# Moving chain links, exponentials and head means of a linear-attention layer by one step in a two-layer transformer kernel

## The reference

```
u_sum = cumsum(u);  bar_u = (log_tau * prior_mu + u_sum) / (log_tau + t)
s_i = -sum(u * bar_u) / sqrt(d)
exp_s = exp(s_i - max(s_i));  E_t = cumsum(exp_s);  P_t = cumsum(s_i)
F_t, G_t, H_t = cumsum(exp_s * k v), cumsum(s_i * k v), cumsum(k v)
M = alpha * F_t + beta * G_t + gamma * H_t      # factors from gate, E_t, P_t
out = q M per head;  out = (out - mean) / sqrt(var + 1e-5);  h = h + out @ Wo.T
```

## Time and profile before

| | us |
|---|---|
| median of 3 runs | 579.2 (577.5 to 581.55) |
| the profiled execution's own time | 581.57 |
| its span, first to last instruction | 579.7 |
| PE busy | 522.0 (90%) |
| PE weight load busy | 495.8 (86%) |
| DVE busy | 382.7 (66%) |
| ACT busy | 256.1 (44%) |
| POOL busy | 226.5 (39%) |

### The profile page before, as it was taken

One profiled execution on the slowest core, in us unless ns is written; L12 is line 12 of the kernel. 1 busy time (PEld: TensorE's weight loads), 2 busy tenths in 40 slices (PEclk: granted clock), 3 DMA queues, 4 the chain that ended last, 5 costly groups with the idle time before them and its releaser, 6 DMA issues. The chain is left out here.

```text
span 579.7 us, 9772 instructions
## 1 busy us (share of the span) xinstructions
PE 522.0 (90%) x3430; PEld 495.8 (86%) x3430; DVE 382.7 (66%) x934; ACT 256.1 (44%) x531; POOL 226.5 (39%) x186
## 2 busy tenths in 40 slices
PE   5799878989999999999999699796687879999996
PEld 5799778989999999999999598585566778999995
DVE  1576748747666666665663966999764766466665
ACT  0347561335455445544651248754631255243432
POOL 1403102746557666765666023774432100021300
PEclk9899967989999999999999899989777799799999
DMA  8740001855566756755743340000202000000001
GB/s 340 258 204 1 2 0 31 320 173 172 180 225 216 276 196 236 253 222 199 246 169 94 97 150 2 0 2 1 75 1 75 1 0 2 2 0 1 2 0 62
DMA packets 22634, 65.03 MB, mean 112 GB/s; under 512 B 6432, under 2 KB 15008, under 8 KB 19776
## 3 DMA queue, kind: packets, MB, share of 16 engines
q1 hardware_dynamic: 20192, 59.55, 29.3%
q0 software_dynamic: 2400, 4.93, 2.5%
HBM read 55.50 MB, written 8.97 MB: 111 GB/s over the span
## 5 line engine op out<-in xcount | busy, mean ns | idle before, releaser
L726 POOL TENSOR_TENSOR w0l<-stage,w0h 128x768 fp32r<-128x768 f32 x34 | 62.5, 1839 | 81.4 <-ACT w0h L710 68.6
L683 PE MATMUL bank<-w0d,a0h 128*128 128x192 f32 x492 | 84.2, 329 | 1.3 <-DVE a0h L765 1.3
L683 PEld LDWEIGHTS bank<-w0d,a0h 128*128 128x128 f32 x492 | 80.8, 192 | 1.6 <-DVE a0h L765 1.6
L758 DVE TENSOR_SCALAR a0t<-bank 128x256 f32<-128x256 f32 (+1 forms) x114 | 50.8, 445 | 41.8 <-PE bank L663 41.5
L737 ACT ACTIVATE bank<-bank 128x256 f32<-128x256 f32 x96 | 35.3, 368 | 84.7 <-PE bank L663 80.7
L663 PE MATMUL bank<-XWh,w0h 128*128 128x256 f32 x192 | 56.1, 292 | 0.0
L663 PE MATMUL bank<-XWh,w0t 128*128 128x256 f32 x192 | 54.5, 284 | 0.0
L663 PE MATMUL bank<-XWh,w0l 128*128 128x256 f32 x192 | 53.9, 281 | 0.0
L663 PE MATMUL bank<-XWl,w0h 128*128 128x256 f32 x192 | 53.9, 281 | 0.0
L663 PE MATMUL bank<-XWl,w0t 128*128 128x256 f32 x192 | 53.9, 280 | 0.0
L446 PE MATMUL bank<-X,w1h 128*128 128x384 f32 x144 | 49.3, 343 | 2.2 <-DVE a1hf L601 2.2
(11 more groups left out here) (256 smaller groups left out, 1302.6 us busy)
## 6 DMA issues: line engine op xcount, KB each, us to landing
stage<-moe0w SPq DMA_DIRECT2D x18, 1536.0 KB, 7.4
w0d<-moe0d SPq DMA_DIRECT2D x18, 576.0 KB, 3.9
stage<-moe1w SPq DMA_DIRECT2D x4, 1056.0 KB, 5.1
marked_rows<-zero SPq DMA_DIRECT2D x4, 772.0 KB, 13.1
patch<-patches SPq DMA_DIRECT2D x4, 768.0 KB, 8.3
XR<-marked_rows SPq DMA_DIRECT2D x16, 192.0 KB, 3.6
G<-slots_out SPq DMA_DIRECT2D x6, 288.0 KB, 4.7
XR<-marked_rows SPq DMA_DIRECT2D x16, 65.0 KB, 3.9
```

The source lines that it names most:

```text
L683: last = nc.tensor.matmul(dst, A0["h"][qpar][:, fc, t * P:(t + 1) * P], W0[par]["down"][:, fc, :], start=(fc == these[0]), stop=(fc == the ...
L726: ins = engine.tensor_tensor(W0[par]["l"][:, mat, :], src, W0[par]["h"][:, mat, :].bitcast(F32), ALU.subtract)
L758: nc.vector.tensor_scalar(A0["t"][fc % 2][:, 0:width], bank[2 + fc % 2][:, 0:width], LIMIT, -LIMIT, ALU.min, ALU.max).then_inc(S0["clip_re ...
```

## The change

Some pieces of the stage stand elsewhere in the step loop; no instruction is added or taken away.

- Chain: `CHAIN` lists us4 ahead of et1 and us5 ahead of cum1. In steps, before: st1 in 0, et1 in 2, us4 in 3, cum1 and us5 in 4, st2 in 5, et2 in 6, cum2 in 7. Now: st1 in 0, us4 in 1, et1 and us5 in 2, cum1 in 3, st2 in 4, et2 in 6, cum2 in 7.
- ACT: `exps(1)` stands in step 1 instead of 2 and `exps(2)` in step 5 instead of 6, each ahead of `centred_squares` and the squares and roots of its step.
- DVE: `masks(g)` stands ahead of `head_variances` and `head_factors` of its step, and `head_means` directly behind `combine`, ahead of key factors, cosines and links.

```diff
-CHAIN = [("us", 0), ("us", 1), ("st", 0), ("us", 2), ("et", 0), ("us", 3), ("cum", 0), ("st", 1), ("et", 1),
-         ("us", 4), ("cum", 1), ("us", 5), ("st", 2), ("et", 2), ("cum", 2)]
+CHAIN = [("us", 0), ("us", 1), ("st", 0), ("us", 2), ("et", 0), ("us", 3), ("cum", 0), ("st", 1), ("us", 4),
+         ("et", 1), ("us", 5), ("cum", 1), ("st", 2), ("et", 2), ("cum", 2)]
-CHAIN_IN = ((7,), (), (8,), (9,), (10, 11), (12,), (13,), (14,))
+CHAIN_IN = ((7,), (8,), (9, 10), (11,), (12,), (), (13,), (14,))
 # ACT, step g
                 out_copies(outs)
+                if g in (1, 5):
+                    exps(g // 5 + 1)
                 if g in (5, 9):
                     centred_squares(g // 4 - 1)
                 if g in (6, 10):
                     head_deviations(g // 4 - 1)
-                if g in (2, 6):
-                    exps(g // 5 + 1)
 # DVE, step g
+                masks(g)
                 if g in (6, 10):
                     head_variances(g // 4 - 1)
                 if g == 7:
                     head_factors(0)
-                masks(g)
 ...
                     combine(g - 1)
+                if g in (4, 8):
+                    head_means(g // 4 - 1)
 ...
                 add_outputs(OUT_AT.get(g, ()))
-                if g in (4, 8):
-                    head_means(g // 4 - 1)
```

## The result

| | before | after |
|---|---|---|
| median, us | 580.12 (12 runs, 575.99 to 581.55) | 576.8 (12 runs, 575.71 to 578.73) |
| the profiled execution's own time, us | 581.57 | 578.16 |
| its span, us | 579.7 | 576.3 |
| mean granted clock | 0.943 | 0.943 |

The ratio is 0.995, with a 95% interval of 0.9929 to 0.9971: 2.9 us are won by the ratio (the medians lie 3.3 apart), and a ratio of 1 lies outside the interval. The forecast was 577.3 us, a gain of 1.9 from the median of 579.2 that was known then.

A forecast was written before the change was run, and what follows sets the result against it. It took DVE's work in steps 2 to 6 as the floor, with at most 4.5 us to win. Its sum, 1.9 us all from the earlier T(8), gave 577.3 us (chance 0.48), range 572.3 to 581.0.

The forecast's parts named there:

- DVE's list up to the cosines: DVE to the cosines of step 4: same work reordered, less a 1.0 us wait, ending at 397.3, 4.9 us later.
- A(5)'s wait: PE in A(5): waits almost 4 us for masks(4), lower clock expected there, all of it hidden.
- POOL and ACT ahead of T(8): POOL's head-mean subtraction ends at 402.0, ACT's copies of group 7 at 406.1; T(8) starts at 406.3, 1.9 us won.
- Where PE stands: PE behind et2: free at 404.1, then waits 2.2 us for T(8).
- A(7) and O(6) at half clock once more: PE behind T(8): its 2.2 us wait makes the clock fall again, and DVE waits for PE in step 7 as before.
- the second case: Rival, chance 0.25: the clock holds at T(8), steps 6 and 7 run at DVE's pace, all 4.5 us won, 574.7 us.
- The size of what could be won: Up to the end of cum2: at most DVE's waits for PE, 1.0 us in step 3 plus 3.5 in step 7, 4.5 us.
- DVE and POOL in each other's way: Rival, chance 0.12: moved DVE instructions meet POOL's work elsewhere and slow down; seven hits would give 582.5 us.
- Masks and head means: DVE: masks(6) lose a 1.7 us delay on which no wait hung; head means ahead of the cosines serve POOL later.
- The tail: Steps 9 and 10: batch 1 head variances cost 0 to 1.1 us, taken as 0; the fall at 439.10 might be spared, 2.8 us.
- the forecast's 419 to 420: Sign of being right: `head_out(0)` starts at 419 to 420 instead of 421.69.

The follow-up runs named there:

- late `head_out`: Changed kernel with the three output transposes of step 8 on PE behind A(8) and O(7), instead of the first ahead of A(8): 572.33 us, ratio 0.9872.

## Why the prediction came near, step by step

The number came near by luck in two places. The step on the clock behind T(8) failed, and an error in the size of what could be won made up for most of it; and the median of before, 579.2 us of three runs when the forecast was made, was 580.12 in the measurement. As gains, 1.9 us were forecast and 2.9 measured. What held is the first half: DVE's list, and where PE waits.

The traces differ by 3.14 us at T(1), so times of after are given less 3.14 to stand beside those of the prediction.

**DVE's list up to the cosines: right.** Forecast end 397.3. The rows of DVE after, where st2 (L1914) follows the cosines and the masks(5) follow st2:

```profile
399.63 0.95 DVE L1945 TENSOR_TENSOR rotA<-QK,const 108x768 f32<-108x768 f32 x1
...
401.42 1.61 DVE L2001 TENSOR_TENSOR AT<-bank,const 108x432 f32<-108x432 f32 x3
```

St2 starts at 400.50, so the cosines end at 397.4; masks(5) start at 398.3 (forecast 398.2). Adding up the old durations less the old wait of 1.0 us was good to 0.1 us over 37 us, since apart from that wait both lists were without a pause.

**A(5)'s wait: right.** 3.98 us, forecast almost 4, with clock 0.51 behind it, hidden. The cosines did come 5.0 us later than in the old order (forecast 4.9), and it did no harm.

**POOL and ACT ahead of T(8): right.** The subtraction of the head means on POOL and the copies of group 7 on ACT:

```profile
403.76 1.51 POOL L1538 TENSOR_TENSOR QK<-QK,HM 108x768 f32<-108x768 f32 x1
```

```profile
405.30 0.84 ACT L1357 ACTIVATE Y<-QK 108x768 f32<-108x768 f32 x1 [3.30 <-POOL QK L1538]
...
407.26 2.06 ACT L1351 ACTIVATE XB<-bank,owner 96x216 f32<-96x216 f32 x6
```

They end at 402.1 and 406.2 (forecast 402.0 and 406.1). T(8) starts at 406.3, as forecast.

**Where PE stands: wrong by 0.8 us.** I had PE free at 404.1 and so waiting 2.2 us; it waited 1.46. A(5) and O(4) at half clock end at 399.8 and push the turns of group 7 in front of A(6), which starts at 400.0 (403.16 in its own time) where the old 0.75 us from masks to scores put it at 399.0. I had counted the half clock at A(5) as hidden from DVE, which it is, but not as shortening PE's next wait.

**"A(7) and O(6) at half clock once more": the step that failed.** Behind T(8) the clock stayed up in both traces of the changed kernel; A(7) took 2.35 us, DVE waited for nothing. So what happened in steps 6 and 7 is the mechanism of the second case, to which I gave 0.25: of the first trace before it takes all (61.96 to 57.28 us, 4.7; that case said 4.5). Only in the trace with late `head_out` did the clock fall there, and it cost 1.4 us.

**The size of what could be won: the second error, and it nearly cancels the first.** The second case with its 4.5 us gives 574.7, 2.1 below what was measured. It fails on the number since its 3.5 us of DVE's waits in step 7 came from a single execution; three executions of the same kernel have 3.5, 0.25 and 1.5. The wait in step 3 was sized too small by the same trace: 1.0 us, and 1.8 and 1.9 in the other two. The two together are 4.5, 2.0 and 3.4 us, 3.3 in the mean. The prediction counted 4.5 us of DVE's waits, took more than half as staying, and got a sum near the mean for neither reason. The measured gain of 2.9 to 4.1 us fits the mean of a loss that comes and goes.

**DVE and POOL in each other's way: present, not decisive.** One sum in that rival is wrong: 577.3 less 1.3 is 576.0, not 575.7. In us5, at its new place beside POOL's rotation of step 2, DVE's last instruction became long; the timeline of DVE after and of POOL after:

```profile
384.08 1.18 DVE L1908 TENSOR_TENSOR ES<-UB,tden 108x12 f32<-108x12 f32 x1
```

```profile
383.42 1.81 POOL L1515 TENSOR_TENSOR QK<-rotA,rotB 108x768 f32<-108x768 f32 x1 [1.12 <-DVE rotA L1945]
```

The same instruction takes 0.17 us in the trace before. The Trainium skill, GPSIMD Engine Reference, section Specifications, says that VectorE's instructions with two SBUF inputs contend with POOL for their shared interfaces; both inputs are in SBUF here, and the trace agrees: the reduction just ahead of it (L1907, one input) ran beside the same POOL instruction in 0.35 us, as in the trace before. cum1 took 4.87 us to the next masks, where it had taken 4.05 to us5. Against it the cosines of step 2 took 0.95 us instead of 1.65, and the query factors of step 3 0.35 instead of 1.17. Hits moved about, the sum stayed: the cosines of step 4 came 0.1 us late and not 1.9.

**Masks and head means: right only with the rest of the change.** I took their cost as zero. With chain and exponentials moved, the time is the same with them and without (0.995 and 0.9954). Alone the masks cost half a per cent. I had priced each move in the company of the others, which the text did not say. That they gain anything in the changed kernel is not shown.

**The tail.** The head variances of batch 1 cost nothing that is seen. `head_out(0)` came 4.7 us earlier from T(1), not the 1.7 to 2.7 us of the forecast's 419 to 420. The 2.36 us ahead of the output product, followed by 1.65 us of slow products in the earlier trace rows, were followed by fast ones after, and the clock fell only 2 us later:

```profile
436.84 0.92 PE L1129 MATMUL bank<-wo_sb,OT 96*128 96x192 f32 x4 [2.36 <-DVE H L2030]
438.20 0.96 PE L1129 MATMUL bank<-wo_sb,OT 96*128 96x192 f32 x4 [0.45 <-DVE H L2030]
438.96 4.03 PE L1087 MATMUL bank<-XB 96*108 96x432 f32 x8
```

That is no merit of the change either: in the second and third traces of before the first row reads 0.92 too, with A(10) at 3.57 and 4.03 us. The first trace before has 39.3 us from `head_out(0)` to L446, the other two 37.0 and 37.6, that after 37.4. Of the 1.8 us by which the first pair differs more at L446 than at `head_out(0)`, 1.1 go with the slow output products (1.4, less 0.3 that A(10) is faster) and 0.7 with O(7), 3.17 us before and 2.45 after.

**What stays open.** What decides behind which wait the clock falls; whether the gains of the change and of the late `head_out` add up; what exps(1), exps(2) or the chain links would win each by itself in the old order, which was not run; and the gain of each part beyond the intervals given.

## What to carry to other kernels

Move work that another engine waits for ahead of work that nobody waits for, in every queue it passes, and move both sides of the dependency: here chain links and exponentials together carried the gain, putting one exponential back lost it, and the move of the masks alone made the kernel slower. An idle engine is worth money only where the one that bounds the stage waits for it; a wait of 4 to 6 us on PE moved from one step to the next without changing the time, as long as DVE worked through. Before trusting a loss read from one trace take a second and third of the same kernel, measured from a common point inside the span: this stage had 62.0, 58.6 and 60.4 us.

## What the runs showed of the hardware

- Whether the clock falls behind a short wait, and how soon, cannot be read off that wait alone. In one and the same kernel, before, 0.79 us ahead of A(6) was followed by half clock in one trace and by full clock in two. Behind the 2.36 us ahead of the output product the clock was low at once in one trace; in the other two that product ran at full clock (0.92 us), and the scores of A(10), 2 to 3 us later, at the lower one (3.57 and 4.03 us against 2.35). In the changed kernel 1.46 and 1.58 us at T(8) were followed by full clock, 1.90 in its variant by 0.52, and in another variant 1.50 us ahead of `head_out(0)` by scores of 4.53 us. Of the waits of 3.7 us and more between step 2 and step 8, in all the traces, each was followed by the lower clock.
- A fall can spare a later one: slow work ahead of a wait makes the wait shorter (0.93 instead of 4.12 us ahead of et2).
- The start of T(1), with the same instructions ahead of it in every kernel here, lay between 357.3 and 366.2 us of the span; that spread is 1.5% of the time, more than the change gains.
- A VectorE instruction of 108x12 took 0.17 us without and 1.18 us beside POOL's work. In these rows the short instruction lost more in proportion than a long one (cosines of 108x768: 0.95 to 1.65 us).
